# Attention steps taken two at a time on TensorE, probabilities in one ring per batch, maxima over 128 rows

## The reference

```
c_adj = mean of x over the channels               # (N)
A     = a function of sigmoid(c_adj[m] - c_adj[n])  # (N, N)
g     = relu(x^T @ (adj * A) * para)               # (C, N): the queries, 4 heads of 64 channels
k, v  = x @ kv_w                                   # keys and values, 4 heads of 64
attn  = softmax(q @ k^T * scale)                   # per head, 1024 x 1024
x1    = layernorm(x + attn @ v)
```

## Time and profile before

| | us |
|---|---|
| median of 3 runs | 3317.03 |
| lowest, highest | 3315.31, 3318.21 |
| the profiled execution's own time | 3317.71 |
| its span, first to last instruction | 3315.9 |
| PE busy | 3002.8 (91%) |
| DVE busy | 2222.7 (67%) |
| ACT busy | 1668.5 (50%) |
| POOL busy | 1077.7 (33%) |

### The profile page before, as it was taken

The page is one execution under the profiler, slowest core; times in us unless marked ns, Lnnn a source line. Parts: engine busy times, 40 slices in busy tenths (PEclk is TensorE's granted clock), DMA queues, the critical chain, the costliest instruction groups (busy, mean ns, idle before and its releaser), DMA issues. The chain is left out here.

```text
span 3315.9 us, 38866 instructions
## 1 busy us (share of the span) xinstructions
PE 3002.8 (91%) x12436; PEld 1845.7 (56%) x12436; DVE 2222.7 (67%) x3015; ACT 1668.5 (50%) x1940; POOL 1077.7 (33%) x500
## 2 busy tenths in 40 slices
PE   6999999999999999999999999999959999997963
PEld 4454545545454544545454554545348888885853
DVE  6677777777687777777687777777543333336877
ACT  5455564546455564546455554646332222225768
POOL 1535243452535244353535344353620000000012
PEclk9999999999999999999999999999979999998986
DMA  4030211213031211213031211213023232325548
GB/s 134 12 115 26 89 57 57 63 51 95 19 114 36 78 57 57 64 50 110 11 107 38 76 57 57 74 40 89 1 95 115 76 114 76 114 75 200 196 154 281
DMA packets 168270, 276.13 MB, mean 83 GB/s; under 512 B 9761, under 2 KB 109089, under 8 KB 168225
## 3 DMA queue, kind: packets, MB, share of 16 engines
q1 hardware_dynamic: 168224, 275.55, 26.2%
HBM read 174.60 MB, written 67.11 MB: 73 GB/s over the span
## 5 line engine op out<-in xcount | busy, mean ns | idle before, releaser
L259 POOL TENSOR_TENSOR psum<-psum,probs 128x1024 f32<-128x1024 f32 x320 | 831.9, 2600 | 245.6 <-ACT probs L324 236.1
L324 ACT ACTIVATE probs<-sc_ps 128x1024 f32<-128x1024 f32 x512 | 524.5, 1024 | 732.2 <-PE sc_ps L786 730.5
L501 DVE TENSOR_REDUCE mx<-mx_ps 128x1 f32<-128x512 f32 x768 | 492.9, 684 | 199.2 <-PE mx_ps L754 197.0
L802 PE MATMUL pv_ps<-probs,v 128*64 128x512 f32 x2048 | 549.9, 615 | 2.8 <-ACT probs L324 2.6
L786 PE MATMUL sc_ps<-qa,ka 128*128 128x512 f32 x1024 | 451.1, 449 | 0.5 <-DVE qb L487 0.5
L786 PE MATMUL sc_ps<-qb,kb 128*128 128x512 f32 x1024 | 405.0, 401 | 0.0
L259 POOL TENSOR_TENSOR psum<-probs 128x1024 f32<-128x1024 f32 x64 | 152.2, 2378 | 757.8 <-ACT probs L324 393.6
L786 PEld LDWEIGHTS sc_ps<-qa,ka 128*128 128x128 f32 x1024 | 194.9, 192 | 291.1 <-issue 173.0
L754 PE MATMUL mx_ps<-ka,qa 64*128 64x512 f32 x768 | 296.3, 452 | 8.2 <-ACT v L312 2.7
L463 DVE SCALAR_TENSOR_TENSOR scr<-scr,adj_ring 128x1024 f32<-128x1024 f32 x128 | 219.8, 1718 | 102.4 <-ACT scr L292 99.9
L718 PE MATMUL sc_ps<-w_hi,x_hi 128*128 128x512 f32 x512 | 222.5, 434 | 59.0 <-DVE w_lo L468 58.6
(11 more groups left out here) (182 smaller groups left out, 5386.4 us busy)
## 6 DMA issues: line engine op xcount, KB each, us to landing
adj_ring<-in_adj_dram SPq DMA_DIRECT2D x128, 512.0 KB, 3.8
pre_scratch<-pre SPq DMA_DIRECT2D x32, 1024.0 KB, 4.2
hid<-pre_scratch SPq DMA_DIRECT2D x32, 1024.0 KB, 5.1
x<-in_x_dram SPq DMA_DIRECT2D x16, 1024.0 KB, 5.6
kb<-ka SPq DMA_DIRECT2D x64, 256.0 KB, 3.0
qa<-qa SPq DMA_DIRECT2D x64, 256.0 KB, 3.3
res<-in_x_dram SPq DMA_DIRECT2D x16, 1024.0 KB, 5.5
x_scratch<-res SPq DMA_DIRECT2D x16, 1024.0 KB, 4.3
```

Of the source, the lines that this page charges most:

```text
L259: pool.tensor_tensor(psum[:, :], probs[:, 0, :] if k == 1 else psum[:, :], probs[:, k % PR, :], ALU.add).then_inc(s["pool_added"], 1)
L324: nc.scalar.activation(probs[:, i % PR, :], sc_ps[:, t % 2, :], ACT.Exp, scale=SCALE)\
L501: nc.vector.tensor_reduce(mx2[:, nh, n:n + 1], mx_ps[:, nh, :], AX.X, ALU.max)\
L802: ins = nc.tensor.matmul(pv_ps[nh * HD:(nh + 1) * HD, h % 2, :], v[:, i, h * HD:(h + 1) * HD], probs[:, i % PR, nh * BANK:(nh + 1) * BANK] ...
```

## The change

Nothing is computed otherwise but the shift of the softmax, which is taken from a better product. The parts:

1. PE takes two steps at a time: S(i) and S(i+1), then V(i-2) and V(i-1). With every S there is an M as long as tiles are left, and one more behind the V's of the first two pairs. TB stands behind S(5), SU before the V's of the pair (2, 3), TS behind them, TM behind the V's of the pair (4, 5). TX and the means stand at the very end of a head, behind V(5), and the key product of head 3 behind S(1).
2. `probs` is one ring over the 32 tiles of a batch: tile t = 8h + i has slot t mod 3. exp(t) waits for the V of tile t-3, and for the add that read tile t-3.
3. On ACT `head_copy` stands before exp(2) and `den_copy` behind exp(3).
4. On DVE `add_last` comes behind three tiles of maxima; then two tiles, the inversion, two tiles, `add_head`, one tile.
5. For heads 1 to 3 M multiplies over 128 rows, high queries by both parts of the keys, and waits for the DMA copy of the queries and the remainder of the keys.

```
-                wait(act, s["pv_done"], 32 * b + t + 1 - (2 if i < 2 else 5 if i == 2 else PR))
-                if i == 1:
-                    wait(act, s["acc_done"], 4 * b + h)
-                elif i != 2:
-                    wait(act, s["pool_added"], POOL_ADDS * (4 * b + h) + (max(1, i - PR) if i else 0))
-                nc.scalar.activation(probs[:, i % PR, :], sc_ps[:, t % 2, :], ACT.Exp, scale=SCALE)\
+                wait(act, s["pv_done"], 32 * b + max(0, t + 1 - PR))
+                prev, tile = divmod(t - PR, T)
+                if t < PR:
+                    wait(act, s["pool_added"], POOL_ADDS * 4 * b)
+                    wait(act, s["acc_done"], 4 * b)
+                elif tile == T - 1:
+                    wait(act, s["acc_done"], 4 * b + prev + 1)
+                else:
+                    wait(act, s["pool_added"], POOL_ADDS * (4 * b + prev) + max(1, tile))
+                nc.scalar.activation(probs[:, t % PR, :], sc_ps[:, t % 2, :], ACT.Exp, scale=SCALE)\
...
-                        if h and i == 1:
+                        if h and i == 2:
                             head_copy(b, h - 1)
                         exponential(b, h, i)
-                        if h and i == SUM_STEP:
+                        if h and i == 3:
                             den_copy(b, h - 1)
...
                 for h in (1, 2):
+                    maxima(b, h + 1, range(0, 3))
                     add_last(b, h - 1)
-                    maxima(b, h + 1, range(0, 3))
+                    maxima(b, h + 1, range(3, 5))
                     invert_sums(b, h - 1)
-                    maxima(b, h + 1, range(3, 6))
+                    maxima(b, h + 1, range(5, 7))
                     add_head(b, h - 1)
-                    maxima(b, h + 1, range(6, T))
+                    maxima(b, h + 1, range(7, T))
                     maxima_row(b, h + 1)
...
-                    wait(pe, s["qh_done"], 4 * b + h + 1)
+                    wait(pe, qa_in[h], 16 * (b + 1))
+                    wait(pe, s["kl_done"], 4 * b + h + 1)
...
-                    nc.tensor.matmul(out, qa[h][own(h), n * P:(n + 1) * P], ka[h][own(h), nh * BANK:(nh + 1) * BANK],
+                    rows = slice(0, P) if h else own(h)
+                    nc.tensor.matmul(out, qa[h][rows, n * P:(n + 1) * P], ka[h][rows, nh * BANK:(nh + 1) * BANK],
...
+                    tiles = T if h + 1 < HEADS else 0
+                    for i in range(0, T, 2):
+                        for k in (i, i + 1):
+                            scores(b, h, k, [1] if h == 0 and i == 0 else (0, 1))
+                            if h and k == 5:
+                                transpose_back(b, h - 1)
+                            if n < tiles:
+                                max_scores(b, h + 1, n, last)
+                                n += 1
+                        if not last and (h, i) == (HEADS - 1, 0):
+                            prepare(b + 1, h, 1)
+                        if h and i == 2:
+                            sum_up(b, h - 1)
+                        if i:
+                            values(b, h, i - 2)
+                            values(b, h, i - 1)
+                        elif h:
+                            values(b, h - 1, T - 2)
+                            values(b, h - 1, T - 1)
+                        if h and i == 2:
+                            transpose_sums(b, h - 1)
+                        if i < 4 and n < tiles:
+                            max_scores(b, h + 1, n, last)
+                            n += 1
+                        if tiles and i == 4:
+                            transpose_maxima(b, h + 1)
+                        if not last and i == T - 2:
+                            prepare(b + 1, h, T - 1)
```

More of the change, by code:

```diff
@@ L62, in attention_layer @@
     WR, DR, AR, PR = 3, 3, 2, 3
[L63 to L66, removed]
     POOL_ADDS = T - 2
@@ L258, in body @@
                         wait(pool, s["exp_done"], 32 * b + 8 * h + k + 1)
-                        pool.tensor_tensor(psum[:, :], probs[:, 0, :] if k == 1 else psum[:, :],
-                                           probs[:, k % PR, :], ALU.add).then_inc(s["pool_added"], 1)
+                        pool.tensor_tensor(psum[:, :], probs[:, 8 * h % PR, :] if k == 1 else psum[:, :],
+                                           probs[:, (8 * h + k) % PR, :], ALU.add).then_inc(s["pool_added"], 1)
             over_batches(pool, B, body)
@@ L516, in add_last @@
                 wait(dve, s["pool_added"], POOL_ADDS * (4 * b + h + 1))
-                nc.vector.tensor_tensor(psum[:, :], psum[:, :], probs[:, (T - 1) % PR, :], ALU.add)\
+                nc.vector.tensor_tensor(psum[:, :], psum[:, :], probs[:, (8 * h + T - 1) % PR, :], ALU.add)\
                     .then_inc(s["acc_done"], 1)
@@ L802, in values @@
                     ins = nc.tensor.matmul(pv_ps[nh * HD:(nh + 1) * HD, h % 2, :], v[:, i, h * HD:(h + 1) * HD],
-                                           probs[:, i % PR, nh * BANK:(nh + 1) * BANK],
+                                           probs[:, t % PR, nh * BANK:(nh + 1) * BANK],
                                            start=i == 0, stop=i == T - 1)
@@ L864, in body @@
                     n = 0
-                    more = h + 1 < HEADS
-                    for i in range(T):
-                        scores(b, h, i, [1] if h == 0 and i < 2 else (0, 1))
-                        if more and MAX_BEFORE[i]:
+                    tiles = T if h + 1 < HEADS else 0
[20 more added lines that the diff above has]
+                        if i < 4 and n < tiles:
@@ L869, in body @@
                             max_scores(b, h + 1, n, last)
                             n += 1
-                        if more and i == ROW_STEP:
+                        if tiles and i == 4:
                             transpose_maxima(b, h + 1)
-                        if not last:
-                            prepare(b + 1, h, i)
-                        if h and i == SUM_STEP:
-                            sum_up(b, h - 1)
-                        if h + i:
-                            values(b, h if i else h - 1, i - 1 if i else T - 1)
@@ L879, in body @@
-                        if more and MAX_AFTER[i]:
-                            max_scores(b, h + 1, n, last)
-                            n += 1
-                        if h and i == DEN_STEP:
-                            transpose_sums(b, h - 1)
-                        if h and i == BACK_STEP:
-                            transpose_back(b, h - 1)
+                        if not last and i == T - 2:
+                            prepare(b + 1, h, T - 1)
+                values(b, HEADS - 1, T - 2)
```

## The result

| | before | after |
|---|---|---|
| median, us (4 runs each, beside each other) | 3317.11 (3315.31 to 3318.21) | 3552.2 (3551.93 to 3553.6) |
| span of the profiled execution, us | 3315.9 | 3550.1 |
| mean granted clock | 0.962 | 0.931 |

The changed kernel takes 1.071 times as long (95%: 1.0692 to 1.0729), 235 us more. The forecast was 3461 us with a range to 3545; 3552 lies 7 us beyond its end. The sign is right. Rival (a), the blocked merge, whose price was 3519, came true, and more of the clock was lost than the sum had.

A forecast was written before the change was run, and what follows sets the result against it. PE's order was taken to set the pace of heads 0 to 2, a DVE remainder head 3's end. Removed work, new waits and lost clock came to +9.3 us a batch, 3317 + 144 = 3461 us, range 3360 to 3545.

The forecast's parts named there:

- Rival (a): Merge of the maxima blocked by POOL's add, TM 2.1 us later in heads 1 and 2: 3519 us; chance 0.25.
- the sum: Heads 0 to 3 change by -2.7, +4.1, +4.4, +3.5: +9.3 us a batch, 15.5 batches, +144 us.
- What bounds the kernel: PE's order sets the pace of heads 0 to 2; head 3's end is set by a DVE remainder.
- The walk of head 1: PE's new order step by step from TX: 22.9 us of work and 6.4 of waits, against 26.4 before.
- the row at 0.18: Profile row: a DVE operation started 0.18 us behind a POOL add and went first; taken as nearest to the merge.
- The row at 0.58: Profile row: the merge started 0.58 us behind a POOL add and took 1.82 instead of some 0.1.
- the clock's term: PE's clock drops after the wait for TS: 1.2 us each in heads 1 and 2, 1.5 in head 3.
- the walk of head 3: Key product now before SU: SU at 10.7, TS at 16.0 us, 3.1 later than before; head +3.5 us.
- The work removed: Attention steps on PE: 54 fewer changes of shape a batch at 0.2 us, 10.8 us a batch, 173 in all.
- M's mean near 400 ns: Sign to look for in the profile: M's mean duration near 400 ns instead of 452.
- (b): Rival: PE's clock stays up through the waits for TS, 60 us less, 3401 us; chance 0.18.
- (c): Rival: in heads 1 and 2 only the wait for TS is left and the clock stays up, 3271 us; chance 0.12.

The follow-up runs named there:

- Experiment 2: The changed kernel with the merge of the maxima as a reduction of one SBUF input instead of two: 3444.6 us.
- experiment 6: The changed kernel with den_copy ahead of exp(3), one-input merge, TX and means before the last two V's, their ACT copy before exp(7): 3265.0 us; M over 64 rows: 3335.2.
- experiment 5: The changed kernel with TX and head 2's means ahead of the head's last two V's, and ACT's copy of their result ahead of exp(7): 3458.5 us.
- experiment 7: Parts alone in the kernel before, ratios: M over 128 rows 0.9916, one-input merge 0.9865, both 0.9756, one ring of probabilities 0.9997.

## Why the prediction was right and wrong

**What bounds the kernel** was right. PE's order sets the pace, and what holds PE is what counts.

**The walk of head 1** was right to a few tenths up to TS. From TX's start it had M(0) at 3.5 with a wait of 1.5, SU at 12.55, TS at 17.9 with a wait of 2.5. Measured: 3.47 and 1.44, 12.27, 17.48 and 2.41. Behind TS it charged 1.2 us of clock, and the V's that it put 4.6 us behind TS come after 5.84. The 48 waits were predicted at about 120 us in all and are 115, the 30 before M(0) are 43.4. PE's work was to be 22.9 us; 26.51 busy less the 3.36 lost to the clock (0.10 of 33.6) is 23.15.

**The step that failed first is the merge** (rival (a) against the sum). The walk had it start 0.2 us behind POOL's add, which was right (0.24). It then let it through, on the row at 0.18, as the nearest. Measured, the merge took 2.12 us, where its one-input form takes 0.17 beside an add, and PE waited 2.84 us before TM where the walk had 0.7. Over all 48 merges the median duration is 2.12 us. The row at 0.58, which I set aside for being further off, was the one that told. The trace of the kernel before had nearer rows that said the same:

```profile
989.56 2.38 POOL L259 TENSOR_TENSOR psum<-psum,probs 128x1024 f32<-128x1024 f32 x1 [0.42 <-ACT probs L324]
...
989.84 3.18 DVE L487 SCALAR_TENSOR_TENSOR qb<-scr,qa 64x1024 fp32r<-64x1024 f32 x1
```

This remainder of the queries, 0.28 behind the add, was blocked, as were 15 more like it; it takes 1.20 us where it goes first. Fourteen products of the first weights (L463), recorded 0.03 behind an add, were blocked too (3.4 us). Only the 16 remainders at 0.17 and 0.18 went first. The rule of the Trainium skill (SBUF — State Buffer, Who interferes with whom) gave the right answer here: two SBUF inputs on VectorE contend with GpSimd's reads for a shared port pair, and the one issued first keeps it. The blocked instruction's record begins before it gets through (the merge's did, by 2.1 us), so recorded starts as close as these do not tell who was first: with POOL's start 0.03, 0.24 and 0.28 us ahead POOL went first, and at 0.18 VectorE did. Rival (a) alone brings the forecast to 3519.

**The second is the clock.** The sum charged 1.2 us in heads 1 and 2 and 1.5 in head 3, all for the waits of TS, 60 us in all, and nothing for TM. Measured, heads 1 and 2 lost 3.4 us each (0.10 of 33.6), about half of it behind TM, whose 4 us ran at 0.57, and head 3 lost none behind TS. TM's part follows from the first failure: at the 0.7 us that the walk gave TM, I saw no cause for it, and the kernel before had lost none behind its 48 waits of 0.85 to 0.88 us there. So the clock's term was 2.2 too small in each of heads 1 and 2 and 1.5 too large in head 3, 2.9 a batch or 45 us, which brings 3519 to 3564, 12 from the measured time. That the two come so close holds some luck, since the sum's other terms are off in both directions (head 3 below). The range treated merge and clock as separate mishaps and left out the case in which both go wrong, but here one made the other. Experiment 2 shows the tie: 108 us came back, of which 64 are the wait before TM, while the lost clock fell by 60 and other waits took some of it back.

**Head 3 and the ends.** Head 0 was 18.4 against a forecast of 18.9. Head 3 was 31.9 against 31.1, but the nearness is luck: 1.5 us of the forecast were clock that was not lost. TS came 16.9 us after the head's start and not 16.0, since SU waited 1.14 us for `head_copy`, which now stands before exp(2); the walk of head 3 did not have that wait. The wait before the next batch's product, which I had folded into head 3, grew by 36 us in all. What made up the rest of the head's excess was not tried. The stretch between batches, costed at no change, is 1.8 us shorter, of which 1.0 is clock.

**The work removed** was counted at 173 us, and 138 are left by subtraction. The two can't be set against each other exactly, since PE's records of M hold waits for maxima, so whether the count or the price of 0.2 us was off is not shown. In head 1 the walk's 22.9 us of work was right (23.15). "M's mean near 400 ns" was wrong, since each record overlaps the next and holds such waits:

```profile
L757 PE MATMUL mx_ps<-ka,qa 128*128 128x512 f32 x768 | 321.1, 469 | 68.1 <-DVE xT_lo L455 43.4 <-DVE mx L501 14.8 <-ACT v L308 2.7
```

**Rivals (b) and (c)** fell. The clock stayed up behind TS in head 3 alone. But (c) named the right condition: over 3.6 us of waits in a head it is slower than before, and with those gone heads 1 and 2 took 24.7 and 25.6 us (experiment 6), near its 25.4.

## What to carry to other kernels

When steps are paired to save on one engine, write down for each small helper (a copy, a merge, a transpose) what now stands between it and its use, and what stands ahead of it in its own engine's queue; here two one-line edits of such helpers were worth 254 us, more than the pairs ever promised. Give a small VectorE operation one SBUF input if GpSimd streams beside it. When the trace has several rows of such a meeting, read them all and not the nearest one. And give a wait on TensorE of 2 us and more a price in clock as a range and not as a number: in these traces the 4 us behind it lost between nothing and 2.0 us.

## What the runs showed of the hardware that I had not expected

- The same wait of PE need not have the same effect on its clock. In the kernel before, the wait of 2.02 us before the transpose of head 0's maxima was followed by a lower clock in 8 of 16 batches, every second one; in experiments 2 and 5 it was in none. The 2.4 us before TS were followed by a lower clock in 30 of 32 cases in heads 1 and 2 after and in 3 of 32 in experiment 5; in head 3 it was 2 of 16 after and 13 of 16 in experiment 5. Behind the waits of 2.8 us before TM it was lower in all 64 cases of these two kernels, and behind the 48 of 0.85 to 0.88 us before, in none. What decides in between is open.
- With M over 64 rows, in head 0 of experiment 6, the granted clock was 0.50 for 4 us in which PE's busy time is 4.00, and in that head no wait of PE longer than 0.39 us stands ahead of it. A wait of 2.03 us, though, ends 2.5 us before the head begins. Low clock sets in 8.2 to 8.7 us behind that wait in 8 of this kernel's 16 batches and never there with 128 rows, where the wait is as long. So the narrower products have a part in it; whether through their shape or through the waits for maxima inside their records was not tried apart.
- A VectorE operation of 0.17 us takes 2.1 if it has two SBUF inputs and a GpSimd add is under way; with one input it runs beside it untouched. In the kernel before, with nothing else touched, this was worth 1.35% (experiment 7, ratio 0.9865).
